# Last layer's probabilities turned by VectorE and SBUF-to-SBUF transfers instead of by TensorE, and new step orders

## The chip, the cores and the metric

The kernel runs on one core of a Trainium2 chip. The metric is the device time of one execution in microseconds; lower is better.

## The reference

64 graphs of 256 nodes with 256 channels go through four layers. All share one 256x256 adjacency matrix. After each layer `x = layernorm(x + layer(x))`. The layers, in short:

```python
# layer 0: scores from two projections
e = leaky_relu((x @ W1) @ (x @ W2).T);  h = relu(softmax(mask(e)) @ (x @ W3))
# layer 1: additive scores
h = x @ W; e = leaky_relu(h @ a1 + (h @ a2).T);  h = elu(softmax(mask(e)) @ h)
# layer 2: MLP, unmasked attention over 512 channels, MLP, masked attention
# layer 3: four heads of 64 channels
q, k, v = x @ wq.T + bq, x @ wk.T + bk, x @ wv.T + bv        # split into 4 heads
scores = where(adj == 0, -inf, q @ k.T / 8)
attn = nan_to_num(softmax(scores));  out = (attn @ v) @ wo.T + bo
```

Layer 3 is the one that changes. Per graph it has four matrices of probabilities of 256x256, one per head. The product `attn @ v` needs each of them with the key index on the partitions, so they have to be transposed.

## The kernel before

Each graph's data lies in tiles of 128 partitions: nodes or channels in two tiles (`NT = CT = 2`). Most products run in three matmuls on a high and a low part (`product3`, lines 192 to 199). Each of the five engines has its own program, and each program is a loop over rounds (`run`, lines 21 to 28). A string per engine in `ORDERS` (lines 8 to 14) lists the steps of a round and for each a stage: in round `k` the step `name:s` works on graph `k - s`. So every step of every layer occurs once per round, for graphs that are at different depths, and some eight graphs are under way at once. Within an engine the steps run strictly in the written order; between engines semaphores hold them back.

The steps of layer 3 for one graph are these.

- TensorE `q4`, `k4`, `v4`: the projections; ScalarE and VectorE make high and low parts in `qT`, `kT`, VectorE adds the bias into `v4`.
- TensorE `s40` and `s42` (lines 403 to 420): scores of heads 0 and 1, then 2 and 3, in PSUM banks 7 and 6.
- VectorE `s40` to `s43` (lines 911 to 917): per head, mask and negated maximum; the result goes to the SBUF tile `p4`, which has room for two heads.
- ScalarE `p40` to `p43` (lines 644 to 651): the exponential with its sum, in place.
- VectorE `p40` to `p43` (lines 919 to 923): reciprocal of the sum. GpSimd `d40` to `d43` and `p40` to `p43` (lines 1029 to 1040): the scaling, in place.
- TensorE `t40` to `t43` (lines 422 to 426): four 128x128 transposes per head into PSUM, through `transposes` (lines 210 to 214).
- ScalarE `t40` to `t43` (lines 653 to 657): copy from PSUM to `p4T`.
- TensorE `a4` (lines 428 to 436): 16 matmuls of `v4` with `p4T` into bank 6, then ScalarE and VectorE `a4`, TensorE `y4` (the output projection), VectorE `y4`, `st4`, `ag4`, GpSimd `v4`, VectorE `n4` (the layer norm) and SyncE `st`, the store.

SyncE issues only three transfers per round: `lt` and `lx` load the input (transposed and plain), `st` stores. All have 128 partitions.

Steps of other layers that are named later: `g0`, `h0`, `s0`, `t0`, `a0`, `x0` (layer 0), `h1`, `f1`, `t1`, `a1`, `x1` (layer 1), `m2`, `n2`, `c2`, `r2`, `f2`, `d2`, `v2`, `b2`, `w2`, `m3`, `n3`, `h3`, `f3`, `t3`, `a3`, `o3`, `x3` (layer 2). The steps `t0`, `t1`, `t3`, `x0`, `x1`, `x3` and `o3` of TensorE are transposes of the same kind as `t40`; `c2` and `r2` (`hidden`, lines 306 to 312) have 24 matmuls each; `f1`, `f3`, `b2` spread two columns, `f2` four.

Of the kernel before, what the change touches and what calls it, by code (L numbers as in the profile page):

```python
# [13 lines left out]
}  # L14
# [16 lines left out]
def graph_stack(nc, x, xT, adj, ident_d, weights, out):  # L31
# [21 lines left out]
    with ExitStack() as ctx:  # L53
# [25 lines left out]
        def small(name, *shape):  # L79
# [42 lines left out]
        nmx4 = sb("nmx4", [P, HEADS, NT])  # L122
        p4 = sb("p4", [P, 2, NT, N])
        p4T = sb("p4T", [P, HEADS, NT, N])
        den4 = sb("den4", [P, HEADS, NT])
# [5 lines left out]
        STAGED = ("W1T", "W2T", "W_T", "hand_T")  # L131
        W.update({n: p4T[:, i, :, :] for i, n in enumerate(STAGED)})
        W.update({"mlp2": p4[:, :, :, :].rearrange("p a b n -> p (a b) n"), "mlp1": o1T[0][:, :, :].rearrange("p (a b) n -> p a (b n)", a=2),
                  "wqT": sco[0][:, :, :], "wkT": sco[1][:, :, :], "wvT": sco[2][:, :, :], "W3": act[0][:, :, :],
# [13 lines left out]
 o3_mm o3T o3Th o3Tl h3_mm h3h h3 f3_mm raw2 nmax2 pro2 rden2 proT2_mm proT2h proT2 av3_mm act2 cut3 ex3 cl3 q3 on3_mm r3 y2 mv2 rstd2 xn2 xnT2_mm xnT2h xnT2  # L148
 q4_mm qTh qT k4_mm kTh kT v4_mm v4 sc4_mm nmx4 p4 rd4a rd4 p4n p4T_mm p4T av4_mm o4Th o4T xb4 y4_mm y3 mv3 rstd3 xn3 stored0 stored1""".split()
        S = {n: ctx.enter_context(nc.semaphore("s_" + n)) for n in names}  # L150
        stored = [S["stored0"], S["stored1"]]
        block = ctx.enter_context(nc.Block())

        def wait(eng, sem, n):
# [5 lines left out]
        @block.sync  # L160
        def _(sp):
            for n, w in weights.items():
                if n not in ("fc", "fc_T"):
                    sp.dma_start(W[n][:, :, :], w).then_inc(S["loaded"], 16)
            for i in range(2):
                sp.dma_start(fc_halves[i], weights["fc"][:, 2 * i:2 * i + 2, :]).then_inc(S["loaded"], 16)
            for k in range(HT):
                sp.dma_start(fcT_tiles[k], weights["fc_T"][:, k, :]).then_inc(S["loaded"], 16)
            sp.dma_start(adj_sb, adj).then_inc(S["loaded"], 16)
            sp.dma_start(ident[:, :], ident_d).then_inc(S["loaded"], 16)  # L170

# [12 lines left out]
            run("sp", {"lt": load_x0T, "lx": load_x0, "st": store}, B)
            sp.wait_ge(stored[0], 16 * ((B + 1) // 2))
            sp.wait_ge(stored[1], 16 * (B // 2))

        @block.tensor
        def _(pe):
# [228 lines left out]
            def s42(t):  # L418
                pe.wait_ge(S["p4T"], HEADS * t + 2)
                scores(2)  # L420

            def t4(h):
                def step(t):
                    pe.wait_ge(S["p4n"], HEADS * t + h + 1)
                    transposes(bank[7 - h % 2], p4[:, h % 2, :, :]).then_inc(S["p4T_mm"], 1)
                return step

            def a4(t):
                pe.wait_ge(S["p4T"], HEADS * t + HEADS)
                for c in range(CT):  # L430
                    for k in range(NT):
                        for g in range(2):
                            h = 2 * c + g
                            ins = nc.tensor.matmul(bank[6][g * HD:(g + 1) * HD, c, :], v4[:, k, h * HD:(h + 1) * HD], p4T[:, h, k, :],  # L434
                                                   start=(k == 0), stop=(k == NT - 1))
                ins.then_inc(S["av4_mm"], 1)

            def y4(t):
# [5 lines left out]
                       "m3": m3, "n3": n3, "h3": h3_, "f3": f3, "t3": t3, "a3": a3, "o3": o3, "x3": x3_, "q4": q4, "k4": k4, "v4": v4_, "s40": s40, "s42": s42,  # L444
                       "t40": t4(0), "t41": t4(1), "t42": t4(2), "t43": t4(3), "a4": a4, "y4": y4}, B)

        @block.scalar
        def _(ac):
# [195 lines left out]
            def p4_(h):  # L644
                def step(t):
                    ac.wait_ge(S["nmx4"], HEADS * t + h + 1)
                    for m in range(NT):
                        ins = nc.scalar.activation(p4[:, h % 2, m, :], p4[:, h % 2, m, :], ACT.Exp, scale=-1.0,  # L648
                                                   bias=nmx4[:, h, m:m + 1], accum_out=den4[:, h, m:m + 1])
                    ins.then_inc(S["p4"], 1)  # L650
                return step

            def t4(h):
                def step(t):
                    ac.wait_ge(S["p4T_mm"], HEADS * t + h + 1)
                    copy(p4T[:, h, :, :], bank[7 - h % 2]).then_inc(S["p4T"], 1)
                return step

            def a4(t):
# [7 lines left out]
                       "q4": q4, "k4": k4, "p40": p4_(0), "p41": p4_(1), "p42": p4_(2), "p43": p4_(3),  # L667
                       "t40": t4(0), "t41": t4(1), "t42": t4(2), "t43": t4(3), "a4": a4}, B)

        @block.vector  # L670
        def _(dv):
# [239 lines left out]
            def s4(h):  # L911
                def step(t):
                    dv.wait_ge(S["sc4_mm"], HEADS // 2 * t + h // 2 + 1)
                    for m in range(NT):
                        ins = V.tensor_tensor_reduce(p4[:, h % 2, m, :], bank[7 - h % 2][:, m, :], mask3[:, m, :], -1.0, BIG, ALU.add, ALU.min, nmx4[:, h, m:m + 1])  # L915
                    ins.then_inc(S["nmx4"], 1)
                return step

            def p4_(h):
                def step(t):  # L920
                    dv.wait_ge(S["p4"], HEADS * t + h + 1)
                    V.reciprocal(den4[:, h, :], den4[:, h, :]).then_inc(S["rd4a"], 1)  # L922
                return step

# [16 lines left out]
            def n4(t):  # L941
                dv.wait_ge(S["rstd3"], 3 * t + 3)
                for m in range(NT):
# [142 lines left out]
```

## Time and profile before

| | us |
|---|---|
| median of 3 runs (lowest, highest) | 3012.59 (3006.74, 3022.74) |
| profiled execution | 3014.59 |
| its span, first to last instruction | 3012.8 |
| TensorE busy | 2812.3 |
| VectorE busy | 2116.2 |
| ScalarE busy | 2101.1 |
| GpSimd busy | 1501.1 |

The mean granted clock of TensorE is 0.98 of full speed. In the lists of groups a row names the line, the engine, the operation, the output and inputs, the shape and the count, then the busy time, the mean duration of one in ns, and the idle time before it with what ended it. The time inside a program that runs for thousands of microseconds is best read in one round of the steady part.

### The profile page before, as it was taken

The page shows a single profiled execution, that of the slowest core. Times are in us where ns is not written, and L with a number is a line of the kernel's source. Part 1 is how long each engine was busy: PE and PEld are TensorE (multiplying, and loading weights), DVE is VectorE, ACT ScalarE, POOL GpSimd, SP SyncE. Part 2 cuts the span into 40 slices and gives each one's busy share as a digit, 9 for nine tenths or more (in the row PEclk, how much of TensorE's full clock was granted, in tenths as well). Part 3 has the DMA queues.
Part 4 walks back from the last instruction along what each step waited for, and adds up shares of the span by engine and source line. Part 5 has one row for each costly group of instructions (what it writes and reads, how often), then busy time and mean ns, then how long its engine had stood idle before and what let it go on. Part 6 is the DMA issues. An engine that isn't in the chain of part 4 may idle for free.

```text
span 3012.8 us, 62503 instructions
## 1 busy us (share of the span) xinstructions
PE 2812.3 (93%) x23496; PEld 2665.5 (88%) x23496; DVE 2116.2 (70%) x5995; ACT 2101.1 (70%) x5057; POOL 1501.1 (50%) x2119
## 2 busy tenths in 40 slices
PE   4689999999999999999999999999999999999886
PEld 3689999999999999999999999999999999998874
DVE  3357777777777777777777777777777777777664
ACT  1367777777777777777777777777777777776663
POOL 0245555555555554555555555555555545554442
PEclk8899999999999999999999999999999999999997
DMA  3000000000000000000000000000000000000000
GB/s 106 22 15 19 15 19 22 22 15 19 22 15 19 22 15 22 19 22 15 19 22 15 19 22 21 16 19 22 16 18 22 15 22 19 22 15 8 8 8 11
DMA packets 40606, 60.98 MB, mean 20 GB/s; under 512 B 4592, under 2 KB 21360, under 8 KB 40304
## 3 DMA queue, kind: packets, MB, share of 16 engines
q1 hardware_dynamic: 40304, 56.98, 5.7%
q8 instruction: 186, 3.05, 0.4%
q14 instruction: 116, 0.95, 0.1%
HBM read 40.19 MB, written 16.78 MB: 19 GB/s over the span
## 4 chain that ended last, share of the span: by engine, by line
PE 84%; DVE 11%; ACT 2%; issue 1%; POOL 1%; SPq 0%; DMA 0%; POOLq 0%; DVEq 0%; ACTq 0%
PE ps L197 41%; PE ps L213 8%; PE ps L206 6%; PE ps L351 6%; PE ps L310 6%; PE ps L311 6%; PE ps L434 4%; DVE xn L944 3%; PE ps L219 2%; PE ps L333 2%; PE ps L409 2%; DVE act L782 2%; DVE o3Tp_lo L675 1%; DVE pfc L817 1%; DVE act L787 1%
## 5 line engine op out<-in xcount | busy, mean ns | idle before, releaser
L963 POOL TENSOR_TENSOR o1Tp_lo<-o1T,o1Tp_hi 128x1024 fp32r<-128x1024 f32 x64 | 162.0, 2531 | 441.1 <-ACT o1Tp_hi L450 441.1
L915 DVE CUSTOM_DVE_ANT_0 p<-ps,mask 128x256 f32<-128x256 f32 x512 | 194.4, 418 | 143.2 <-PE ps L409 143.2
L1032 POOL TENSOR_TENSOR rd<-some,den 128x2 f32<-128x2 f32 x256 | 87.2, 340 | 395.9 <-DVE den L922 395.7
L1038 POOL TENSOR_TENSOR p<-p,rd 128x512 f32<-128x512 f32 x256 | 267.1, 1043 | 15.6
L648 ACT ACTIVATE p<-p,nmx 128x256 f32<-128x256 f32 x512 | 255.0, 505 | 10.2 <-DVE nmx L915 10.2
L717 DVE CUSTOM_DVE_ANT_0 sco<-ps,mask 128x256 f32<-128x256 f32 x384 | 145.8, 417 | 134.8 <-ACT ps L453 134.8
L450 ACT ACTIVATE xnT_hi<-ps 128x512 fp32r<-128x512 f32 x192 | 115.7, 603 | 178.4 <-PE ps L213 178.4
L975 POOL TENSOR_SCALAR xn<-act,nmean,rstd 128x256 f32<-128x256 f32 x384 | 210.7, 558 | 29.6 <-POOL rstd L970 22.4
L213 PE MATMUL ps<-ident,sco 128*128 128x128 f32 x768 | 123.4, 284 | 75.9 <-ACT sco L458 75.6
L458 ACT ACTIVATE sco<-sco,nmax 128x256 f32<-128x256 f32 x384 | 191.3, 517 | 3.6 <-DVE nmax L717 3.6
L675 DVE TENSOR_TENSOR xnT_lo<-ps,xnT_hi 128x512 fp32r<-128x512 f32 x192 | 130.6, 680 | 81.7 <-ACT xnT_hi L450 81.5
L970 POOL TENSOR_TENSOR rstd<-vare,mhalf 128x2 f32<-128x2 f32 x256 | 181.8, 710 | 0.0
L996 POOL TENSOR_TENSOR act<-act,xn 128x512 f32<-128x512 f32 x64 | 88.8, 1387 | 174.7 <-DVE act L782 174.7
L213 PEld LDWEIGHTS ps<-ident,sco 128*128 128x128 f32 x768 | 83.7, 141 | 100.6 <-ACT sco L458 92.5
L450 ACT ACTIVATE h_hi<-ps 128x512 fp32r<-128x512 f32 x192 | 113.8, 593 | 83.9 <-PE ps L206 49.4
L213 PE MATMUL ps<-ident,p 128*128 128x128 f32 x1024 | 156.8, 276 | 15.7 <-POOL p L1038 15.7
L450 ACT ACTIVATE p4T<-ps 128x512 f32<-128x512 f32 x256 | 153.9, 603 | 12.3 <-PE ps L213 12.3
L197 PE MATMUL ps<-xnT_lo,w_mlp_hi 128*128 128x256 f32 x512 | 155.3, 303 | 6.3 <-ACT o1T L539 3.4
L453 ACT ACTIVATE ps<-ps,cols 128x256 f32<-128x256 f32 x384 | 155.4, 450 | 3.0 <-PE ps L219 3.0
L450 ACT ACTIVATE hfc_hi<-ps 128x512 fp32r<-128x512 f32 x128 | 76.5, 598 | 113.0 <-PE ps L311 113.0
L967 POOL TENSOR_TENSOR vare<-mv,eps 128x2 f32<-128x2 f32 x256 | 49.9, 195 | 205.9 <-DVE mv L729 205.9
L197 PE MATMUL ps<-pfcp_lo,hfc_hi 128*128 128x256 f32 x512 | 150.9, 295 | 0.0
(250 smaller groups left out, 12968.1 us busy)
## 6 DMA issues: line engine op xcount, KB each, us to landing
x0T<-in_xT SPq DMA_DIRECT2D x64, 256.0 KB, 3.0
x<-in_x SPq DMA_DIRECT2D x64, 256.0 KB, 2.7
out<-xn SPq DMA_DIRECT2D x64, 256.0 KB, 2.2
o1T<-in_mlp SPq DMA_DIRECT2D x1, 512.0 KB, 4.7
p<-in_mlp SPq DMA_DIRECT2D x1, 512.0 KB, 4.6
att<-in_fc SPq DMA_DIRECT2D x1, 512.0 KB, 5.3
ex<-in_fc SPq DMA_DIRECT2D x1, 512.0 KB, 6.3
xn<-in_fc_T SPq DMA_DIRECT2D x2, 256.0 KB, 6.5
```

What stands on the lines that cost most here:

```text
L197: ins = nc.tensor.matmul(dst[:, m, :], lhs[a][:, k, (off + m) * P:(off + m + 1) * P], rhs[b][:, k, :], start=(k == 0 and i == 0), stop=(k ...
L206: ins = nc.tensor.matmul(dst[m][:, 0:C2], lhs[a][:, k, m * P:(m + 1) * P], rhs[b][:, k, :], start=(k == 0 and i == 0), stop=(k == CT - 1 a ...
L213: ins = nc.tensor.transpose(dst[:, b, a * P:(a + 1) * P], src[:, a, b * P:(b + 1) * P], ident[:, :])
L310: nc.tensor.matmul(ps[:, 4, 0:C2], lhs, WP["fc"][b][:, k, 0:C2], start=(k == 0 and i == 0), stop=(k == HT - 1 and i == 2))
L311: ins = nc.tensor.matmul(ps[:, 5, 0:C], lhs, WP["fc"][b][:, k, C2:], start=(k == 0 and i == 0), stop=(k == HT - 1 and i == 2))
L450: return nc.scalar.activation(dst, src, ACT.Copy)
L458: ins = nc.scalar.activation(sco[i][:, m, :], sco[i][:, m, :], ACT.Exp, scale=-1.0, bias=nmax[i][:, m:m + 1], accum_out=den[i][:, m:m + 1])
L648: ins = nc.scalar.activation(p4[:, h % 2, m, :], p4[:, h % 2, m, :], ACT.Exp, scale=-1.0, bias=nmx4[:, h, m:m + 1], accum_out=den4[:, h, m ...
L915: ins = V.tensor_tensor_reduce(p4[:, h % 2, m, :], bank[7 - h % 2][:, m, :], mask3[:, m, :], -1.0, BIG, ALU.add, ALU.min, nmx4[:, h, m:m + 1])
L970: G.tensor_tensor(rstd[i][:, :], vare[i][:, :], mhalf[:, :], ALU.pow).then_inc(s_rs, 1)
L975: ins = G.tensor_scalar(xn[:, m, :], y[:, m, :], nmean[i][:, m:m + 1], rstd[i][:, m:m + 1], ALU.add, ALU.mult)
L1038: G.tensor_tensor(p4[:, h % 2, :, :], p4[:, h % 2, :, :], rd4[:, h, :].unsqueeze(2).broadcast_to([P, NT, N]), ALU.mult).then_inc(S["p4n"], 1)
```

## The change

Heads are handled in pairs, with one `p4` tile per pair. Within a tile the data is laid out in four blocks of 256 columns, one per quarter of the key index. VectorE transposes all 32x32 blocks of such a tile in place with one instruction (steps `x40` and `x42`, 128x1024 values each). Sixteen transfers issued by SyncE (`i40` and `i42`) then move the 32 partitions of quarter `q`, column block `w`, to the partitions of quarter `w`, column block `q`, of `p4T`. Each moves 32 rows of 1 KB. TensorE's `t40` to `t43` and ScalarE's `t40` to `t43` are gone. TensorE's `s42` waits for the maxima of heads 0 and 1, `a4` for the transfers of each pair. Matmuls and elementwise steps read and write through rearranged views. The orders of all five engines are new.

```diff
 ORDERS = {
-    "sp": "st:9 lx:1 lt:0",
-    "pe": "t3:6 a0:1 s42:7 a3:6 o3:6 d2:5 g0:0 b2:5 v2:5 w2:5 t42:7 x1:4 h0:0 t43:7 m2:4 a4:7 s0:0 x3:6 n2:4 y4:7 q4:6 h1:3 k4:6 m3:5 n3:5 f1:3 x0:2 v4:6 c2:4 s40:6 t1:3 h3:5 t0:0 r2:4 f3:5 t40:6 a1:3 f2:4 t41:6",
+    "sp": "lt:0 i40:7 st:9 lx:1 i42:7",
+    "pe": "h3:8 a0:3 v4:9 f3:8 x0:5 g0:2 s40:9 d2:7 x1:6 t3:8 s42:9 v2:7 a3:8 m2:6 h0:2 b2:7 n2:6 o3:8 w2:7 s0:2 h1:5 c2:6 f1:5 t0:2 a4:9 r2:6 t1:5 x3:8 y4:9 m3:7 n3:7 a1:5 f2:6 q4:8 k4:8",
+    "ac": "t0:3 r2:7 x3:9 m3:8 o3:8 a1:6 f2:7 q4:9 k4:9 h3:8 w2:7 x2:7 a0:3 u3:8 x0:5 p3:8 g0:2 p40:9 t3:8 x1:6 p41:9 p42:9 a3:8 p43:9 m2:6 b3:8 b2:7 h0:2 n2:6 o2:6 s0:2 h1:5 y2:7 p0:2 c2:6 k2:7 u1:5 a4:9 p1:5 z2:7 l0:1 t1:5",
+    "dv": "e0:1 st3:7 h1:4 st0:2 n2:6 ag3:7 ag0:2 c2:5 i2:6 e1:4 j2:6 a4:8 z2:6 x3:7 i1:4 t1:4 i0:1 ag4:9 y4:8 r2:5 t0:1 f2:5 st4:8 b1:4 a1:4 b2:5 q4:7 st1:4 ag1:4 h3:6 k4:7 v4:7 e3:6 x0:3 s40:7 s41:7 g0:0 p40:7 t3:6 s42:7 x1:4 p41:7 i3:6 s43:7 p42:7 d2:5 n4:9 c3:6 p43:7 x40:7 b3:6 h0:0 x42:7 a3:6 r3:6 v2:5 z3:6",
+    "po": "n1:5 d40:8 p40:8 d41:8 p41:8 d42:8 p42:8 d43:8 p43:8 m2:5 a0:2 v3:7 n3:7 v0:2 l0:0 k4:8 v4:9 m3:6 y1:4 n0:2 v1:4 w2:5",
...
-        p4 = sb("p4", [P, 2, NT, N])
-        p4T = sb("p4T", [P, HEADS, NT, N])
+        p4 = [sb(f"p4_{i}", [P, QUADS, 2 * NT * CT * P // QUADS]) for i in range(2)]
+        p4T = sb("p4T", [P, 2, QUADS, 2 * NT * CT * P // QUADS])
+        p4v = [p4[i][:, :, :].rearrange("p w (g a b j) -> p g a w b j", g=2, a=NT, b=CT) for i in range(2)]
+        p4Tv = p4T[:, :, :, :].rearrange("p c q (g a b i) -> p c g b a q i", g=2, a=NT, b=NT)
...
+            def turn_in(c):
+                def step(t):
+                    sp.wait_ge(S["p4x"], 2 * t + c + 1)
+                    wait(sp, S["av4_mm"], t)
+                    for w in range(QUADS):
+                        for q in range(QUADS):
+                            sp.dma_start(p4T[w * QP:(w + 1) * QP, c, q, :], p4[c][q * QP:(q + 1) * QP, w, :]).then_inc(p4Tin[c], 16)
+                return step
...
             def s42(t):
-                pe.wait_ge(S["p4T"], HEADS * t + 2)
+                pe.wait_ge(S["nmx4"], HEADS * t + 2)
                 scores(2)
 
-            def t4(h):
-                def step(t):
-                    pe.wait_ge(S["p4n"], HEADS * t + h + 1)
-                    transposes(bank[7 - h % 2], p4[:, h % 2, :, :]).then_inc(S["p4T_mm"], 1)
-                return step
-
             def a4(t):
-                pe.wait_ge(S["p4T"], HEADS * t + HEADS)
+                pe.wait_ge(S["nmx4"], HEADS * t + HEADS)
                 for c in range(CT):
+                    pe.wait_ge(p4Tin[c], 16 * QUADS * QUADS * (t + 1))
                     for k in range(NT):
                         for g in range(2):
                             h = 2 * c + g
-                            ins = nc.tensor.matmul(bank[6][g * HD:(g + 1) * HD, c, :], v4[:, k, h * HD:(h + 1) * HD], p4T[:, h, k, :],
+                            ins = nc.tensor.matmul(bank[6][g * HD:(g + 1) * HD, c, :], v4[:, k, h * HD:(h + 1) * HD], p4Tv[:, c, g, k, :, :, :],
...
             def s4(h):
                 def step(t):
                     dv.wait_ge(S["sc4_mm"], HEADS // 2 * t + h // 2 + 1)
+                    wait(dv, p4Tin[h // 2], 16 * QUADS * QUADS * t)
...
+            def turn4(c):
+                def step(t):
+                    dv.wait_ge(S["p4n"], HEADS * t + 2 * c + 2)
+                    V.transpose(p4[c][:, :, :], p4[c][:, :, :]).then_inc(S["p4x"], 1)
+                return step
```

## Rows read from the trace of the kernel before

**Rows 1.** The page: busy time by engine, and the chain that ended last.
```profile
PE 2812.3 (93%) x23496; PEld 2665.5 (88%) x23496; DVE 2116.2 (70%) x5995; ACT 2101.1 (70%) x5057; POOL 1501.1 (50%) x2119
...
PE 84%; DVE 11%; ACT 2%; issue 1%; POOL 1%; SPq 0%; DMA 0%; POOLq 0%; DVEq 0%; ACTq 0%
```

**Rows 2.** Busy time in a stretch: PE, PEld, DVE, ACT, POOL, clock, DMA share, GB/s.
```profile
400.00:2400.00 2000.00, 1942.03 (x16562) 1851.88 (x16562) 1480.69 (x4214) 1482.54 (x3581) 1065.39 (x1496) 1.00 0.06 19
```

**Rows 3.** The chain in order of time, one round: start us, us, what.
```profile
1499.39 0.91 PE ps L409 x12
...
1506.30 1.42 PE ps L197 x12
...
1509.97 1.63 DVE xn L944 x2
...
1514.98 1.02 PE ps L333 x8
...
1522.84 0.44 PE ps L213 x4
...
1524.71 1.88 PE ps L434 x16
1526.59 1.61 PE ps L197 x12
...
1535.80 2.82 PE ps L351 x24
1538.62 0.22 PE ps L219 x2
...
1543.57 0.91 PE ps L409 x12
```

**Rows 4.** TensorE's instructions in order of time: start, us, then the idle time before.
```profile
1509.63 0.66 PE L213 MATMUL ps<-ident,sco 128*128 128x128 f32 x4 [1.03 <-ACT sco L458]
```

**Rows 5.** The page's costliest groups, those of layer 3's probabilities.
```profile
L915 DVE CUSTOM_DVE_ANT_0 p<-ps,mask 128x256 f32<-128x256 f32 x512 | 194.4, 418 | 143.2 <-PE ps L409 143.2
...
L1038 POOL TENSOR_TENSOR p<-p,rd 128x512 f32<-128x512 f32 x256 | 267.1, 1043 | 15.6
L648 ACT ACTIVATE p<-p,nmx 128x256 f32<-128x256 f32 x512 | 255.0, 505 | 10.2 <-DVE nmx L915 10.2
...
L213 PE MATMUL ps<-ident,p 128*128 128x128 f32 x1024 | 156.8, 276 | 15.7 <-POOL p L1038 15.7
L450 ACT ACTIVATE p4T<-ps 128x512 f32<-128x512 f32 x256 | 153.9, 603 | 12.3 <-PE ps L213 12.3
```

**Rows 6.** VectorE's groups by shape, 1500 to 2100 us: those of 128x1024.
```profile
L836 DVE SCALAR_TENSOR_TENSOR att<-att,o1T 128x1024 f32<-128x1024 f32 x13 | 15.8, 1215 | 0.0
...
L832 DVE TENSOR_SCALAR ex<-ex 128x1024 f32<-128x1024 f32 x14 | 10.0, 712 | 7.4 <-ACT ex L575 7.4
```

**Rows 7.** SyncE's queue: duration of issues (min/median/max), their starts, landing.
```profile
L178 SPq DMA_DIRECT2D x<-in_x x64: 327/328/609, 17.8 to 2719.9; - x64
L182 SPq DMA_DIRECT2D out<-xn x64: 372/395/403, 274.6 to 3010.2; - x64
...
11.41 0.43 SPq L164 DMA_DIRECT2D w_m<-in_m  x1
11.88 0.43 SPq L166 DMA_DIRECT2D att<-in_fc  x1
12.36 0.43 SPq L166 DMA_DIRECT2D ex<-in_fc  x1
...
1527.29 0.33 SPq L178 DMA_DIRECT2D x<-in_x  x1
1527.66 0.43 SPq L174 DMA_DIRECT2D x0T<-in_xT  x1
...
out<-xn SPq DMA_DIRECT2D x64, 256.0 KB, 2.2
...
w_m<-in_m SPq DMA_DIRECT2D x1, 0.5 KB, 4.3
```

More of the change, by code:

```diff
@@ L46, in graph_stack @@
     HD = C // HEADS
+    QUADS = 4
+    QP = P // QUADS
     MASK = -(2.0 ** 100)
@@ L131, in graph_stack @@
         STAGED = ("W1T", "W2T", "W_T", "hand_T")
-        W.update({n: p4T[:, i, :, :] for i, n in enumerate(STAGED)})
-        W.update({"mlp2": p4[:, :, :, :].rearrange("p a b n -> p (a b) n"), "mlp1": o1T[0][:, :, :].rearrange("p (a b) n -> p a (b n)", a=2),
+        p4T_flat = p4T[:, :, :, :].rearrange("p c q n -> p (c q n)").rearrange("p (h t n) -> p h t n", h=HEADS, t=CT)
+        W.update({n: p4T_flat[:, i, :, :] for i, n in enumerate(STAGED)})
+        W.update({"mlp2": p4[0][:, :, :], "mlp1": o1T[0][:, :, :].rearrange("p (a b) n -> p a (b n)", a=2),
                   "wqT": sco[0][:, :, :], "wkT": sco[1][:, :, :], "wvT": sco[2][:, :, :], "W3": act[0][:, :, :],
@@ L148, in graph_stack, with by_quads @@
  o3_mm o3T o3Th o3Tl h3_mm h3h h3 f3_mm raw2 nmax2 pro2 rden2 proT2_mm proT2h proT2 av3_mm act2 cut3 ex3 cl3 q3 on3_mm r3 y2 mv2 rstd2 xn2 xnT2_mm xnT2h xnT2
- q4_mm qTh qT k4_mm kTh kT v4_mm v4 sc4_mm nmx4 p4 rd4a rd4 p4n p4T_mm p4T av4_mm o4Th o4T xb4 y4_mm y3 mv3 rstd3 xn3 stored0 stored1""".split()
+ q4_mm qTh qT k4_mm kTh kT v4_mm v4 sc4_mm nmx4 p4 rd4a rd4 p4n p4x p4T0 p4T1 av4_mm o4Th o4T xb4 y4_mm y3 mv3 rstd3 xn3 stored0 stored1""".split()
         S = {n: ctx.enter_context(nc.semaphore("s_" + n)) for n in names}
         stored = [S["stored0"], S["stored1"]]
+        p4Tin = [S["p4T0"], S["p4T1"]]
         block = ctx.enter_context(nc.Block())
+        def by_quads(row):
+            return row.rearrange("p (b w j) -> p w b j", b=CT, w=QUADS)
         def wait(eng, sem, n):
@@ L182, in store @@
                 sp.dma_start(out[t].rearrange("(t p) c -> p t c", p=P), xn3[t % 2][:, :, :]).then_inc(stored[t % 2], 16)
-            run("sp", {"lt": load_x0T, "lx": load_x0, "st": store}, B)
+            def turn_in(c):
[6 more added lines that the diff above has]
+                return step
+            run("sp", {"lt": load_x0T, "lx": load_x0, "st": store, "i40": turn_in(0), "i42": turn_in(1)}, B)
             sp.wait_ge(stored[0], 16 * ((B + 1) // 2))
@@ L408, in scores @@
                             rows_ = slice((g % 2) * HD, (g % 2) * HD + HD)
-                            ins = nc.tensor.matmul(bank[7 - g % 2][:, m, :], qT[a][rows_, g // 2, m * P:(m + 1) * P], kT[b][rows_, g // 2, :],
+                            ins = nc.tensor.matmul(bank[7 - g % 2][:, m, :], qT[a][rows_, g // 2, m * P:(m + 1) * P], by_quads(kT[b][rows_, g // 2, :]),
                                                    start=(i == 0), stop=(i == 2))
@@ L444, in _ @@
                        "m3": m3, "n3": n3, "h3": h3_, "f3": f3, "t3": t3, "a3": a3, "o3": o3, "x3": x3_, "q4": q4, "k4": k4, "v4": v4_, "s40": s40, "s42": s42,
-                       "t40": t4(0), "t41": t4(1), "t42": t4(2), "t43": t4(3), "a4": a4, "y4": y4}, B)
+                       "a4": a4, "y4": y4}, B)
         @block.scalar
@@ L647, in step @@
                     for m in range(NT):
-                        ins = nc.scalar.activation(p4[:, h % 2, m, :], p4[:, h % 2, m, :], ACT.Exp, scale=-1.0,
+                        rows_ = p4v[h // 2][:, h % 2, m, :, :, :].rearrange("p w b j -> p w (b j)")
+                        ins = nc.scalar.activation(rows_, rows_, ACT.Exp, scale=-1.0,
                                                    bias=nmx4[:, h, m:m + 1], accum_out=den4[:, h, m:m + 1])
                     ins.then_inc(S["p4"], 1)
[L651 to L656, printed above, removed]
                 return step
@@ L667, in _ @@
                        "q4": q4, "k4": k4, "p40": p4_(0), "p41": p4_(1), "p42": p4_(2), "p43": p4_(3),
-                       "t40": t4(0), "t41": t4(1), "t42": t4(2), "t43": t4(3), "a4": a4}, B)
+                       "a4": a4}, B)
         @block.vector
@@ L678, in _ @@
             V.tensor_scalar(mask16[:, :, :], adj_sb, 0.0, MASK, ALU.is_le, ALU.mult)
-            V.tensor_scalar(mask3[:, :, :], adj_sb, 0.0, MASK, ALU.is_equal, ALU.mult).then_inc(S["setup_dve"], 1)
+            for m in range(NT):
+                ins = V.tensor_scalar(mask3[:, m, :].rearrange("p (w b j) -> p w b j", w=QUADS, b=CT), by_quads(adj_sb[:, m, :]), 0.0, MASK, ALU.is_equal, ALU.mult)
+            ins.then_inc(S["setup_dve"], 1)
             dv.wait_ge(S["setup_dve"], 1)
@@ L913, in step @@
                     dv.wait_ge(S["sc4_mm"], HEADS // 2 * t + h // 2 + 1)
+                    wait(dv, p4Tin[h // 2], 16 * QUADS * QUADS * t)
                     for m in range(NT):
-                        ins = V.tensor_tensor_reduce(p4[:, h % 2, m, :], bank[7 - h % 2][:, m, :], mask3[:, m, :], -1.0, BIG, ALU.add, ALU.min, nmx4[:, h, m:m + 1])
+                        ins = V.tensor_tensor_reduce(p4v[h // 2][:, h % 2, m, :, :, :].rearrange("p w b j -> p w (b j)"), bank[7 - h % 2][:, m, :].rearrange("p (w n) -> p w n", w=QUADS),
+                                                     mask3[:, m, :].rearrange("p (w n) -> p w n", w=QUADS),
+                                                     -1.0, BIG, ALU.add, ALU.min, nmx4[:, h, m:m + 1])
                     ins.then_inc(S["nmx4"], 1)
@@ L950, in _ @@
                        "q4": q4, "k4": k4, "v4": v4_, "s40": s4(0), "s41": s4(1), "s42": s4(2), "s43": s4(3),
-                       "p40": p4_(0), "p41": p4_(1), "p42": p4_(2), "p43": p4_(3), "a4": a4, "y4": y4, "st4": st4, "ag4": ag4, "n4": n4}, B)
+                       "p40": p4_(0), "p41": p4_(1), "p42": p4_(2), "p43": p4_(3), "x40": turn4(0), "x42": turn4(1), "a4": a4, "y4": y4, "st4": st4, "ag4": ag4, "n4": n4}, B)
         @block.gpsimd
@@ L1037, in step @@
                     po.wait_ge(S["rd4"], HEADS * t + h + 1)
-                    G.tensor_tensor(p4[:, h % 2, :, :], p4[:, h % 2, :, :], rd4[:, h, :].unsqueeze(2).broadcast_to([P, NT, N]),
-                                    ALU.mult).then_inc(S["p4n"], 1)
+                    rows_ = p4v[h // 2][:, h % 2, :, :, :, :].rearrange("p a w b j -> p a w (b j)")
+                    G.tensor_tensor(rows_, rows_, rd4[:, h, :].unsqueeze(2).unsqueeze(3).broadcast_to([P, NT, QUADS, CT * QP]), ALU.mult).then_inc(S["p4n"], 1)
                 return step
```

3 rows, old and new, of the table ORDERS are left out of this document.

## The prediction

> **What bounds the kernel now.** I read four views. First the page: TensorE is busy for 93% of the span and carries 84% of the chain that ended last, VectorE 11% of it [rows 1]. Then a long stretch from the middle: in 2000 us TensorE is busy for 1942 us and VectorE for 1481, ScalarE for 1483, GpSimd for 1065, at a granted clock of 1.00, the 2.4 GHz level [rows 2]. So this is TensorE's queue with three engines at some three quarters, and what counts is one round: the time from one graph's `s40` to the next one's, 1499.39 to 1543.57, is 44.2 us [rows 3]. 64 rounds are 2828 us; the other 185 us of the 3012.8 us span are the setup and the rounds at both ends.
>
> The same rows give the price of each TensorE step: a product of 12 matmuls 1.43 us (1.42 to 1.61 with what precedes it), a step of four transposes 0.44, a pair of columns spread 0.22, `d2` 1.02, the scores of a pair of heads 0.91, `a4` 1.88, `m3` with `n3` 2.82. A `hidden` step is 24 matmuls of 0.12 us, 2.9 us. One round without a wait is then 14 products 20.0, `h1` and `h3` 2.9, `m3`/`n3` 2.8, `c2` and `r2` 5.8, scores 1.8, `a4` 1.9, eleven transposing steps 4.8, spreads 1.1, `d2` 1.0: 42.1 us. The remaining 2.1 us are waits, such as 1.03 us of `t1` for the exponentials [rows 4], and a stretch of the chain that runs over VectorE's `n4` at 1509.97 [rows 3].
>
> **What the change removes.** `t40` to `t43` on TensorE: four steps of 0.44 us, 1.8 us per round (all 1024 transposes together are 156.8 us busy, with overlaps [rows 5]). That work is on the path. The four copies of 0.60 us on ScalarE [rows 5] go too; ScalarE is at 74%, so by themselves they bring nothing. The round's TensorE work is then 40.3 us. If nothing waited, 3.9 us per round would be gone, 8%.
>
> **What it adds on VectorE.** Two transposes over 128x1024 float32. No row shows one. The nearest rows of the same size are 0.71 us (one tensor and a scalar) and 1.22 us (two tensors) [rows 6]. I take 1.2, as each element is moved at least once; the ends are 0.7 and 2.4 (two passes). VectorE goes from 33 to 35.4 us busy per round, still under 40.3. The Trainium skill, Vector Engine (DVE) Microarchitecture Reference, section 3.8, says that the array sustains one element per cycle per lane; by that the estimate stays at the row of one element per cycle. No run here shows it yet.
>
> **What it adds on the queue of SyncE.** 32 transfers per round of 32 rows by 1 KB, 1 MB in all; the 16 DMA engines are 6% busy [rows 2], so bytes are no matter. What matters is that one queue issues them one after another. The trace has three prices for an issue: a load alone 0.328 us (64 times), a store alone 0.395 (64 times), and `x0T` right behind `x` 0.37 from start to start; in the setup, with a queue of some twenty, 0.475 from start to start, whether 0.5 KB or 512 KB are moved [rows 7]. So size is not what costs. Fewer rows might: the store has twice the rows of the load (1 KB pieces against 2 KB) and costs 0.07 more, by which a quarter of the rows would take 0.05 off, 0.32 with the gap of 0.045. I take 0.40 us per transfer, between 0.37 and 0.475 and nearer the lower end; bounds 0.32 and 0.475. Sixteen take 6.4 us. Landing: the store of 256 KB takes 2.2 us from issue [rows 7]; 32 KB should be a little quicker, 2.0 (1.8 to 2.2).
>
> **The step that decides: from `s42` to `a4`.** `a4` waits for `i40`'s transfers before its first half and for `i42`'s before its second. Both halves hang on `s42` of the same graph in the same round of TensorE's order, so no earlier start of the round absorbs a delay. Time 0 is the end of `s42`.
> VectorE: it is by then through `s40`, `s41`, `g0` and `t3`; masked maximum of head 2 (0.42 us each half [rows 5], 0.7 us per head with overlap) done at 1.0.
> ScalarE: finishes `p41` at 1.15, `p42` (two exponentials of 0.505 [rows 5] and the sums, 0.98) at 2.1. Then `a3` stands in its queue, which needs TensorE's `v2` and `a3`, 2.9; it is done at 3.7. `p43` at 4.7.
> VectorE: `n4` (1.63 [rows 3]), `c3`, reciprocal of head 3 at 4.9; only then `x40`, although its input (GpSimd's 1.04 us products [rows 5]) is ready at about 3.1. `x40` ends at 6.1. `x42`, behind `b3` and `h0`, ends at 8.6.
> SyncE: `i40` issues from 6.1 to 12.5; `st` and `lx`, 0.8 with their gaps, to 13.3; `i42` starts its last transfer at 13.3 + 15 x 0.40 = 19.3, landed at 21.3. `x42` isn't the limit; the queue is.
> TensorE reaches `a4` after `v2 a3 m2 h0 b2 n2 o3 w2 s0 h1 c2 f1 t0`: eight steps of 12 matmuls 11.4, `c2` 2.9, two spreads 0.4, two transposing steps 0.9, 15.6; the second half starts 0.9 later, at 16.5. The first half's transfers land at 6.1 + 6.0 + 2.0 = 14.1 and are in time. The second half waits 21.3 - 16.5 = 4.8 us.
> The other new waits cost nothing by this: `s42` waits for the maxima of heads 0 and 1 instead of two copies; VectorE's `s40` to `s43` wait for the transfers of the graph before to have read `p4`, done some 20 us earlier; SyncE's wait in `i40` holds `st`, `lx` and `i42` behind it, all of which have slack except `i42`. The setup's mask in two instructions is below 1 us, once.
> Behind the wait of `a4` stand, on TensorE, `r2`, `t1`, `x3`, `y4`; on ScalarE `a4`, and behind it `p1`, `z2`, `l0`; on VectorE `a4`, `z2`, `x3`. I followed them round with the same prices: `p1` is done 1.7 us after `a4`, hidden by `r2` (2.9); `t1` on VectorE is done before `a1`; `z2` just before `m3`. No second wait of more than some tenths comes out; the closest are `s42` behind the maxima of heads 0 and 1 and `c2` behind GpSimd's `m2`. `lt` of the next graph goes out right after `i42`, at about 20.3, lands at 23.3, and `l0` comes on ScalarE at about 25: hidden by 2 us; without that cover it would hold `t1`.
>
> **The sum.** Round: 40.3 + 4.8 = 45.1 us against 44.2, +0.9 us; 64 rounds, +58. In the last two rounds TensorE has few other steps and the new path, some 8 us longer than copies behind transposes, lies open: +15. The profiled execution took 3014.6 us (span 3012.8; the median of three is 3012.6): 3014.6 + 73 = about 3090 us.
> With an issue at 0.37 the wait is 3.9 and the round 44.2: 3030. At 0.475 and a landing of 2.2: `i42` starts at 14.5, lands at 23.8, wait 7.3, round 47.6: 3245. At 0.32 and 1.8: 18.6, wait 2.1, round 42.4: 2914. The break-even of a round is 0.37 us per transfer.
>
> **Rivals.**
> A. *Issues are cheap for small transfers.* If cost followed the rows moved, 32 of 128 rows would cost 0.43 / 4 = 0.11 us, `i42` would start with `x42`'s end at 8.7 and land at 12.4, before 16.5. The round is 40.3 plus half of today's waits, 41.4: -2.8 x 64 + 15, 2850 us. Against it: 0.5 KB costs as much as 512 KB, and 256 pieces little more than 128 [rows 7]. For it: no row has 32 partitions. The Trainium skill, DMA: Bandwidth & Descriptors, section Issuing engines are not separate DMA queues, calls the sequencer's time to initiate a DMA "usually small relative to the DMA itself"; by that this rival is right, while the 0.4 us beside 2.2 here, sixteen times, speaks against it. The same page's Rules for kernel authors say that transfers under 64 KB pay mostly overhead and should be joined; by that my forecast is right. Chance 0.15; a middle case, 0.2 to 0.35 us per issue, 2860 to 2990 us, 0.10.
> B. *VectorE becomes the bound.* At 2.4 us per transpose `x40` ends 1.2 later and the issues with it: round 46.3, 3165 us. It decides from the point where `x42` and the steps behind it (`a3 r3 v2 z3 e0`) reach ScalarE's `p0` later than `t0`, which has some 0.5 us to spare, so also by contention of GpSimd with transposes. Chance 0.08, slower.
> C. *The matmuls pay for the new layout.* `s40`, `s42` and `a4` now read their moving side in runs of 32 floats. At half as much again, 0.9 + 0.9 us: 1.8 per round on TensorE, 0.9 of it hidden in the wait; about 3150. Nothing in the trace speaks for it. Chance 0.03. That the change doesn't take the transposes off TensorE can't be: the steps are gone.
> D. The forecast, 0.64: 0.37 to 0.475 us per issue, 3030 to 3245, and a small part below.
>
> **Chances and range.** Measurable is about 0.5%, 15 us. Faster: A 0.15, the middle case 0.09, a part of D 0.02, 0.26. Within 0.5%: 0.08, the lower end of D and 0.01 of the middle. Slower: the rest of D 0.55, B and C 0.11, 0.66. The range leaves out the cheapest issues below (A) and 0.475 with more waits above: 2890 to 3250. Likeliest, by D alone, 3030 to 3245.
>
> **What would show it.** In the profile after: the distance between two issues of `i40` (0.40 us) and from the last issue to its landing (2.0); the wait of the matmul with `v` and `p4T` for a transfer, about 4.8 us in each round, and a share of it in the chain with DMA and SyncE's queue; VectorE's transpose 1.2 us; rounds of 45.1 us; granted clock 1.00 as before. The prediction is wrong if `a4` doesn't wait (issues under 0.3 us), if `x40` ends much later than 6 us after `s42`, or if another step waits longer than `a4`.

## The result, and the profile after

The kernel after takes 3749.84 us (median of 4 runs, 3745.8 to 3753.1) against 3015.49 us. The ratio is 1.244, 95% interval 1.240 to 1.247: 24% slower, far outside 2890 to 3250. The direction was forecast; the size was not.

The page of the kernel after: busy time, granted clock, and the chain that ended last by engine and by line.

```profile
span 3746.8 us, 62818 instructions
PE 2823.9 (75%) x22472; PEld 2641.0 (70%) x22472; DVE 2282.2 (61%) x6124; ACT 1998.7 (53%) x4801; POOL 1552.0 (41%) x2119
...
PE 50%; SPq 34%; issue 5%; DVE 4%; ACT 3%; DMA 3%; POOL 1%; POOLq 0%; DVEq 0%
SPq L201 32%; PE ps L217 23%; PE ps L371 5%; PE ps L330 4%; PE ps L233 4%; PE ps L449 3%; PE ps L331 3%; DMA p4T<-p 3%; PE ps L429 3%; PE ps L226 2%; DVE p L943 2%; ACT p L664 2%; PE ps L353 2%; PE ps L239 1%; SPq L193 1%
...
L449 PE MATMUL ps<-p4T,v 128*64 128x256 f32 x1024 | 210.8, 551 | 814.8 <-DMA p4T<-p 814.8
```

TensorE had 84% of the chain in [rows 1]; now the queue of SyncE has 34%, nearly all of it in one line, the issue of the small transfers (L201). The last line says what TensorE pays: before `a4` it waits 814.8 us for these transfers, 12.7 us per round. TensorE's own instructions in the round shown next split this wait over the two halves of `a4`; the first half waits too:

```profile
1642.69 1.48 PE L449 MATMUL ps<-p4T,v 128*64 128x256 f32 x8 [2.79 <-DMA p4T<-p]
1653.84 1.98 PE L449 MATMUL ps<-p4T,v 128*64 128x256 f32 x8 [9.68 <-DMA p4T<-p]
```

The chain in order of time, one round, answers to [rows 3] (columns: start, us, what):

```profile
1623.13 0.91 PE ps L429 x12
1624.03 3.06 PE ps L217 x24
...
1627.49 0.47 ACT act L633
1627.96 0.98 ACT p L664 x4
1628.97 0.17 DVE den L937
1629.13 1.15 DVE p L943
1630.30 0.51 SPq L201
1630.86 0.59 SPq L201
1631.49 0.59 SPq L201
...
1636.85 1.29 SPq L201
...
1641.34 0.58 SPq L193
1641.97 0.47 SPq L189
...
1651.33 0.59 SPq L201
1651.97 1.83 DMA p4T<-p
1653.84 1.98 PE ps L449 x8
...
1659.39 0.87 PE ps L233 x8
```

This is the path of the prediction, step by step: scores of `s42` to 1624.03, then `v2` and `a3`, ScalarE's `a3` and `p43`, the reciprocal, `x40`, sixteen issues, store and load, sixteen issues, one landing, `a4`. `x40` ends 6.3 us after `s42`; 6.1 was forecast. But an issue lasts 0.59 us, 0.635 from start to start, not 0.40; 37 of the 2048 last over 1 us. The second half of `a4` starts 29.8 us after `s42`, not at 21.3.

The same stretch by windows (busy PE, PEld, DVE, ACT, POOL; granted clock; DMA share; GB/s):

```profile
1624.00:1641.00 17.00, 15.90 (x134) 15.66 (x132) 13.83 (x35) 11.86 (x31) 6.95 (x8) 1.00 0.11 29
1641.00:1654.00 13.00, 1.63 (x10) 0.76 (x12) 5.45 (x15) 1.85 (x3) 5.81 (x9) 0.59 0.33 89
1654.00:1658.00 4.00, 4.00 (x22) 2.86 (x23) 0.69 (x1) 2.13 (x6) 0.00 (x0) 0.64 0.19 54
1658.00:1679.00 21.00, 21.00 (x188) 20.57 (x188) 15.06 (x44) 15.02 (x37) 11.33 (x16) 1.00 0.01 2
```

While TensorE waits, its granted clock falls from 2.4 to 1.2 GHz, and it still runs at the lower level for the first steps after the wait (0.64 in the third window). The eight matmuls of `a4` take 1.98 us there, and 16 took 1.88 in [rows 3]. [Rows 2] had 1.00.

A mean round is used below. It is the mean of 50 rounds from the middle: the start of `a4`'s second half of the 56th graph less that of the 6th, over 50. In the kernel after these are 3322.28 and 542.38, so 55.6 us; in the kernel before 2674.30 and 465.26, so 44.2. (The last rounds, in which the first layers have nothing left to do, are shorter and are left out.) Over the same 50 rounds the second half of `a4` starts 29.5 us after `s42` in the kernel after, 28.9 to 30.3.

### The profile page after: what moved, and what is told of

It is laid out like the page before. It is cut to its first block, busy times and chain, and to the rows that moved or that the text cites. A ratio compares the mean times of both kernels' runs of the same rounds, so it can differ in the third digit from the quotient of the medians.

```text
span 3746.8 us, 62818 instructions
## 1 busy us (share of the span) xinstructions
PE 2823.9 (75%) x22472; PEld 2641.0 (70%) x22472; DVE 2282.2 (61%) x6124; ACT 1998.7 (53%) x4801; POOL 1552.0 (41%) x2119
## 4 chain that ended last, share of the span: by engine, by line
PE 50%; SPq 34%; issue 5%; DVE 4%; ACT 3%; DMA 3%; POOL 1%; POOLq 0%; DVEq 0%
SPq L201 32%; PE ps L217 23%; PE ps L371 5%; PE ps L330 4%; PE ps L233 4%; PE ps L449 3%; PE ps L331 3%; DMA p4T<-p 3%; PE ps L429 3%; PE ps L226 2%; DVE p L943 2%; ACT p L664 2%; PE ps L353 2%; PE ps L239 1%; SPq L193 1%
## 5 line engine op out<-in xcount | busy, mean ns | idle before, releaser
L449 PE MATMUL ps<-p4T,v 128*64 128x256 f32 x1024 | 210.8, 551 | 814.8 <-DMA p4T<-p 814.8
L449 PEld LDWEIGHTS ps<-p4T,v 128*64 128x64 f32 x1024 | 90.0, 184 | 898.0 <-DMA p4T<-p 671.4
L735 DVE BATCH_NORM_STATS2 stat<-act 128x6 f32<-128x256 f32 x384 | 143.9, 416 | 419.8 <-POOL act L1006 414.8
L465 ACT ACTIVATE qT_hi<-ps 128x512 fp32r<-128x512 f32 x64 | 38.3, 598 | 486.8 <-PE ps L449 486.8
L594 ACT ACTIVATE ex<-ex,w_m 128x1024 f32<-128x1024 f32 x64 | 73.5, 1148 | 419.9 <-DVE ex L844 419.9
L984 POOL TENSOR_TENSOR x0Tp_lo<-x0T,x0Tp_hi 128x512 fp32r<-128x512 f32 x64 | 111.9, 1749 | 434.8 <-ACT x0Tp_hi L465 434.8
L1006 POOL TENSOR_TENSOR act<-act,x 128x512 f32<-128x512 f32 x64 | 81.4, 1271 | 496.6 <-DMA x<-in_x 486.3
L988 POOL TENSOR_TENSOR vare<-mv,eps 128x2 f32<-128x2 f32 x256 | 107.9, 422 | 412.7 <-DVE mv L741 412.7
L685 DVE TENSOR_TENSOR qT_lo<-ps,qT_hi 128x512 fp32r<-128x512 f32 x64 | 44.3, 692 | 379.1 <-ACT qT_hi L465 379.1
L330 PE MATMUL ps<-w_fc_lo,o1Tp_hi 128*128 128x258 f32 x512 | 177.6, 347 | 8.5 <-POOL o1Tp_lo L984 5.9
```

The costliest lines, as they stand in the source:

```text
L330: nc.tensor.matmul(ps[:, 4, 0:C2], lhs, WP["fc"][b][:, k, 0:C2], start=(k == 0 and i == 0), stop=(k == HT - 1 and i == 2))
L984: return G.tensor_tensor(lo, whole, hi.bitcast(fp32), ALU.subtract)
```

## The experiments

A run that is given without a ratio was executed once.

**One transfer of sixteen.** The wait at `a4` is the suspect; this takes away what it waits for.

```diff
-for w in range(QUADS):
-    for q in range(QUADS):
-        sp.dma_start(...)
+for i in range(1):          # eight in the second run; waits count accordingly
+    w, q = i // QUADS, i % QUADS
+    sp.dma_start(...)
```

> Kernel after with one of the sixteen transfers of each pair of heads (30 of the 32 per round left out, so most of p4T keeps old values); transposes, new orders and new views stay. Theory Q (the wait of a4 for SyncE's 16 + 16 issues at 0.635 us from start to start makes the slowdown): the second pair is landed at about 9 + 0.6 + 1.8 = 11.4 us after s42, before a4 needs it at 16.5; rounds of 40.3 to 41.5 us, granted clock 1.00, about 2840 to 2910 us. Rival V (VectorE's transposes, the new order or matmuls that read in runs of 32 are slow by themselves): it stays above 3015 us, with another wait or longer matmuls.

Measured: 2800.28 us, ratio to before 0.928 (0.923 to 0.934). In the steady part TensorE has no idle time left (the columns are those of [rows 2]):

```profile
800.00:2400.00 1600.00, 1600.00 (x13745) 1539.26 (x13745) 1375.47 (x3739) 1226.66 (x2954) 971.01 (x1295) 1.00 0.08 22
```

The mean round is 40.8 us, 0.5 more than the prediction's sum of TensorE's steps and with no wait in it; a matmul of `a4` takes 0.379 us as in the kernel before. Transposes on VectorE, new orders, and matmuls that read in runs of 32 cost nothing on the path; rival V falls. The whole loss comes with the other 30 transfers.

**Eight of sixteen.**

> Kernel after with eight of the sixteen transfers per pair (half of p4T keeps old values). Theory Q: i40 issues from 6.25 to 11.3, st and lx to 12.5, the last of i42 starts at 16.9 and lands at 18.7, a wait of 2.2 us at a4: rounds of 42.5 to 43.5 us, 2980 to 3040 us. Rival V: hardly different from the run with one transfer.

3047.06 us, just above the range named; mean round 44.7 us. The wait at `a4` is 2.4 us per round in the middle, against 2.2 expected. The clock makes most of the rest: it is 0.96 in the steady part, and the expectation had left it out. From the start of `a4`'s second half to the steps of L233 it is 5.2 us in the mean, against 3.9 in the run with one transfer. In 36 of the 50 rounds this stretch is over 5 us, behind waits of only 1.8 to 3.1 us; in the other 14 it is 4.0.

**What sets the price of an issue: fewer bytes, more partitions.** Two runs change the shape alone.

```diff
-p4T[w*QP:(w+1)*QP, c, q, :],      p4[c][q*QP:(q+1)*QP, w, :]
+p4T[w*QP:(w+1)*QP, c, q, 0:64],   p4[c][q*QP:(q+1)*QP, w, 0:64]      # 32 rows of 256 B
+p4T[:, c, q, w*64:(w+1)*64],      p4[c][:, w, q*64:(q+1)*64]         # 128 rows of 256 B
```

> Kernel after, all 32 transfers per round, but each of its 32 rows is 256 bytes instead of 1 KB (three quarters of p4T keep old values). If an issue has a price per instruction: still 0.59 us each, about 3750 us. If the price follows the bytes: under 0.3 us each, landing under 1.8, rounds near 41 us, about 2870 us. If only the landing shrinks: some 20 us less.

> Kernel after, all 32 transfers per round with the same 32 KB each, but as 128 rows of 256 bytes over all partitions (the blocks don't go to their places, so the output is of wrong probabilities). If the 32-partition shape is what makes an issue 0.59 us instead of the 0.43 us of the loads in the setup: 0.43 us each, 0.475 from start to start, a wait of about 7 us, 3250 us. If it is that both ends lie in SBUF, or that many follow one another: 0.59 us, about 3750 us. If more rows cost more: above 3750 us.

3746.96 and 3758.67 us. The issues in the first, the second, and for comparison the run with one transfer (durations in ns, min/median/max):

```profile
L201 SPq DMA_DIRECT2D p4T<-p x2048: 507/591/1935, 243.2 to 3730.2; - x187
```
```profile
L201 SPq DMA_DIRECT2D p4T<-p x2048: 464/601/1748, 243.9 to 3741.8; - x187
```
```profile
L193 SPq DMA_DIRECT2D out<-xn x64: 378/584/1440, 322.2 to 2793.4; - x64
L201 SPq DMA_DIRECT2D p4T<-p x128: 507/513/1301, 240.1 to 2781.1; - x128
```

A quarter of the bytes, 0.591 us as in the kernel after; four times the rows and partitions, 0.601. So it is a price per instruction. Nor is it the length of the queue: with a single transfer per pair it is 0.51 us, and the store right behind it takes 0.58, against 0.395 in [rows 7].

**The same transfers with one end in device memory.**

```diff
-p4[c][q*QP:(q+1)*QP, w, :]
+xT[t][q*QP:(q+1)*QP, c, :]
```

> Kernel after with the same 32 transfers of 32 rows by 1 KB to the same places in p4T, but read from the input in device memory instead of from p4 (so the probabilities are left out of the product). Theory E (an issue whose both ends lie in SBUF costs 0.59 us, one with an end in device memory 0.43): 0.475 us from start to start; i40 from 6.25 to 13.9, st and lx to 14.9, the last of i42 starts at 22.0 and lands near 24.4, a wait of 7.9 us and the lower clock behind it, rounds of 48.5 to 50 us, 3300 to 3400 us. If it is the number of rows or partitions: 0.59 us and 3750 us as after.

3426.62 us; the issues in the same form, and the first of a round by time:

```profile
L201 SPq DMA_DIRECT2D p4T<-in_xT x2048: 310/421/1952, 242.5 to 3409.9; - x187
```
```profile
1607.06 0.31 SPq L201
1607.41 0.42 SPq L201
1607.88 0.42 SPq L201
...
1623.28 1.70 DMA p4T<-in_xT
1625.02 1.97 PE ps L449 x8
...
1631.81 0.87 PE ps L233 x8
```

0.42 us instead of 0.59, 0.465 from start to start, with the same 32 rows to the same places. What makes an issue dear here is that both its ends lie in SBUF. The time is a little above the range named: mean round 50.4 us. From the start of `a4`'s second half to the steps of L233 it takes 6.8 us in the round shown and 6.1 in the mean of the 50 (5.4 to 6.9), where a full clock needs 3.9 to 4.0 (below). The lower clock costs 2.2 us per round here.

**Keeping the clock up.** 90 matmuls stand ahead of the second wait.

```diff
+if c == 1:
+    for _ in range(90):
+        nc.tensor.matmul(bank[6][:, 1, :], WP["wvT"][0][:, 0, 0:P], WP["wvT"][0][:, 1, :], start=True, stop=True)
 pe.wait_ge(p4Tin[c], 16 * QUADS * QUADS * (t + 1))
```

> Kernel after with 90 matmuls of 256 columns put in front of a4's wait for the second pair (their result is overwritten, so the output is kept). They take 10.6 us in which TensorE otherwise waits. Theory C (besides the wait of 12.7 us per round, TensorE's clock falls behind each wait and costs another 1.8 us: rounds of 55.3 us less 12.7 are 42.6, while the run with one transfer has 40.8): clock 1.00, rounds of about 53.5 to 54 us, 3630 to 3670 us. If the 1.8 us are other waits: 3750 us as after, or more.

3719.34 us, ratio to before 1.234 (1.231 to 1.237), so 31 us below the kernel after, not 80 to 120. The chain:

```profile
1630.51 1.83 DMA p4T<-p
...
1632.48 1.08 PE ps L452 x8
1633.56 10.98 PE ps L447 x90
1644.55 1.01 PE ps L452 x8
...
1648.62 0.87 PE ps L233 x8
```

The eight matmuls behind the fill take 1.01 us instead of 1.98, and 4.1 us pass until the steps of L233 where the round shown of the kernel after needs 5.5. That round is one of the mild ones: from start to start the stretch is 4.0 us in each of the 50 rounds with the fill and 6.0 in the mean of the kernel after (5.4 to 6.9). So the clock costs 2.1 us per round there. But the first half of `a4` itself waited for its transfers until 1632.48, and the fill started late. The matmuls behind it started 0.3 us after the last transfer's landing in this round and 1.0 in the mean (0.04 in the kernel after), and the issues of the second pair took 0.4 us longer than in the kernel after, so that the mean round fell by only 0.7 us, to 54.9. The price of the clock is shown by the rows; its gain in this run is smaller by the overshoot and the issues.

**The two issues between the pairs.**

```diff
-"sp": "lt:0 i40:7 st:9 lx:1 i42:7"
+"sp": "lt:0 lx:1 i40:7 i42:7 st:9"
```

> Computes the full result. Kernel after with SyncE's order changed alone: lx before i40 and st behind i42, so that nothing stands between the 32 issues. Theory Q: every round loses the 1.2 us of these two issues from the chain: 54.1 us, about 3675 us. If the queue is not the chain, no change from 3750. VectorE's long idle stretch behind GpSimd's wait for x (7.8 us per round) should go as well; if that was what cost, more than 1.2 us per round goes.

3695.03 us, 55 below the kernel after, where 75 were expected; the mean round is 54.6, 1.0 less. The second half of `a4` starts 1.1 us earlier, by the length of the two issues, and the stretch at the lower clock behind it is 0.1 longer. Two issues that leave the queue between the pairs give nearly their own length, as a queue on the path must. `stat L735 <- POOL act`, up to 7.8 us per round in the middle and 414.8 us in all, went out of VectorE's waits and gave nothing of its own; VectorE's wait for `qT_hi` grew from 379 to 731 us.

**More cover for the same 32 transfers.**

```diff
 "pe": ... t0:2 r2:6 t1:5 x3:8 m3:7 n3:7 a4:9 a1:5 f2:6 y4:9 q4:8 k4:8    # a4 7 us later
 "ac": t0:3 r2:7 x3:9 m3:8 o3:8 a4:10 a1:6 f2:7 ...                       # a4 moved to the start of the next round
 "dv": ... p42:7 d2:5 x40:7 n4:9 c3:6 p43:7 ...                           # x40 ahead of n4; a4, y4, st4 later
 "sp": lt:0 lx:1 i40:7 i42:7 st:9                                         # first run
 "sp": lt:0 lx:2 i40:8 i42:8 st:10                                        # second: all but lt a stage later, so lt a round earlier than the rest
```

> Computes the full result. All 32 transfers as in after, but more cover: TensorE's a4 moved behind r2, t1, x3, m3, n3 (7 us later in the round), y4 behind f2, VectorE's x40 ahead of n4 (1.8 us earlier), SyncE as in the run with its order changed. Theory Q: i40 issues from 4.4 to 15.2 us after s42, the last of i42 starts at 24.7 and lands at 26.5; a4's second half could start at 23.4: a wait of 3.1 us and the lower clock behind it, rounds of 44 to 46 us, 3000 to 3130 us, no better than before. If it stays above 3500 us, the number of issues isn't what holds it.

3478.5 us, not 3000 to 3130, and just below the 3500 above which the number of issues would not have been what holds it. `a4` hardly waits any more (59.7 us in all), but something else does. Its chain, from the last issues on:

```profile
1660.39 0.59 SPq L201
1660.99 0.04 issue
1661.03 0.58 SPq L193
1661.62 0.04 issue
1661.66 2.67 DMA x0T<-in_xT
...
1664.89 0.58 ACT proT_hi L465
...
1667.73 0.60 DVE proT_lo L685
1668.32 0.04 issue
1668.37 2.93 PE ps L217 x12
```

The load of `x0T` stands behind the 32 issues. ScalarE's `l0` waits for it and holds `t1`, `a1` waits for that. This is the cover of 2 us that the prediction named at `l0`; with `a4` off the path it is used up. The second run puts the load ahead.

> Computes the full result. The kernel with the later a4, and the load of x0T one round earlier in SyncE's order, so that it goes out before i40 and not behind the 32 issues. In the run before, the chain went from the last issue over the landing of x0T (2.7 us), ScalarE's queue and VectorE's proT and xnT back to TensorE, and a4 waited only 60 us in all. If that is the whole reason why later didn't reach 3000 to 3130 us: it does now, with a4's wait of about 3 us per round back. If VectorE or ScalarE is out of order for another reason: it stays above 3300 us.

3097.74 us, inside 3000 to 3130 at the second attempt. The remaining waits are not where they were expected: 60.8 us at `a4`, 96.1 for `o2T` and 61.5 for `hfc`, 3.4 us per round together; the mean round is 45.0. So with the same 32 transfers the kernel is 24% or 3% slower than the kernel before, by where their consumer and the load behind them stand.

**Fewer issues, through device memory.** This computes the whole result.

```diff
+def turn_out(c):            # i40, i42
+    sp.dma_start(scratch[c], p4[c][:, :, :]).then_inc(p4out[c], 16)
 def turn_in(c):             # j40, j42, after p4out[c]
     for w in range(QUADS):
-        for q in range(QUADS):
-            sp.dma_start(p4T[w*QP:(w+1)*QP, c, q, :], p4[c][q*QP:(q+1)*QP, w, :]).then_inc(p4Tin[c], 16)
+        sp.dma_start(p4T[w*QP:(w+1)*QP, c, :, :], scratch[c][:, w, :].rearrange("(q j) n -> j q n", q=QUADS)).then_inc(p4Tin[c], 16)
-"sp": "lt:0 i40:7 st:9 lx:1 i42:7"
+"sp": "lt:0 i40:7 st:9 lx:1 i42:7 j40:7 j42:7"
```

> Computes the full result. Kernel after, but the blocks of a pair change places through device memory: one transfer of 128 partitions writes the turned tile out, four transfers of 32 partitions read it back, 10 issues per round instead of 32, with one landing more in the way (2.5 and 2.9 us). Theory Q (number of issues, not bytes or distance): i42 goes out at 8.9 us after s42, has landed at about 11.5, the last read starts at about 13.5 and lands at 16.4, just when a4 needs it at 16.5. Rounds of 40.8 to 41.5 us, 2800 to 2850 us, against 3015 before. If the round trip through device memory takes over 2 us more than that: a wait and a lower clock again, over 2950 us. It also shows whether an issue between device memory and SBUF with 32 partitions costs 0.43 or 0.59 us.

2873.41 us, ratio to before 0.954 (0.951 to 0.956), a little above the 2800 to 2850 named. A read back costs 0.43 us again behind another. What is left of the wait at `a4` is 82.5 us, since the landings are longer than assumed (us from issue to landing, last column):

```profile
scratch<-p SPq DMA_DIRECT2D x128, 512.0 KB, 3.4
p4T<-scratch SPq DMA_DIRECT2D x512, 128.0 KB, 3.5
```

**The same with two changes of order.**

```diff
-"sp": "lt:0 i40:7 st:9 lx:1 i42:7 j40:7 j42:7"
+"sp": "lt:0 lx:1 i40:7 i42:7 j40:7 j42:7 st:9"
-"dv": "... x40:7 b3:6 h0:0 x42:7 a3:6 ..."
+"dv": "... x40:7 b3:6 x42:7 h0:0 a3:6 ..."
```

> Computes the full result. The kernel through device memory with two changes of order: VectorE turns the second pair ahead of h0 (x42 some 1.2 us earlier after s42), and SyncE issues lx ahead of i40 and st last, so that the load of x doesn't stand between the two writes. Theory Q: the 1.2 us that a4 still waited per round go: rounds near 40.5 us, 2800 to 2830 us. If s0 now waits for the late h0, or the landings stay at 3.4 and 4.2 us because the bytes of both pairs meet on the DMA engines: 2840 to 2880 us, hardly better than 2873.

2823.45 us, ratio to before 0.936 (0.934 to 0.938), mean round 41.0. It is the fastest kernel of this study that computes the whole result, and 23 us above the run with one transfer, the bound for this path. TensorE is busy all but 6 of 1600 us:

```profile
800.00:2400.00 1600.00, 1593.71 (x13659) 1530.08 (x13658) 1378.62 (x3708) 1217.51 (x2926) 967.11 (x1290) 1.00 0.23 72
```

## Why the prediction was right and wrong

**Right: what is removed, and nearly what the round is without waits.** 40.3 us per round was the sum of TensorE's steps; the run with one transfer has 40.8.

**Right: the place and the path.** The wait that sets the round is at `a4`'s second half, the limit is SyncE's queue and not `x42`, `x40` ends at 6.3 us (6.1), the landing is 1.8 us (2.0), VectorE's transpose 1.23 us (1.2). Rivals B and C are excluded by the run with one transfer, rival A by every trace here. That the first half would be in time was wrong: it waits 2.3 us per round. This costs nothing by itself, as the second half's transfers land some 11 us later still.

**Wrong: the price of an issue.** This is the step that failed. 0.40 us, with bounds 0.32 and 0.475, was taken from transfers of [rows 7] that all have one end in device memory. The rows fit those, as the run from memory shows: 0.465. With both ends in SBUF it is 0.635. The argument that a quarter of the rows would take 0.05 us off gave nothing: a quarter of the bytes left the price where it was, and four times the rows and partitions added 0.01. None of the prediction's three signs of being wrong came true either; they looked at a cheaper issue, a late `x40` and another step, and not at a dearer issue. A term that enters the path 31 times should have had a bound from outside the kinds of transfer that the trace happened to show, and break-even lay at 0.37.

**Wrong: the clock was left out.** A wait of this length lets the granted clock fall to 1.2 GHz, and the work behind it pays: 2.1 us per round here, 2.2 in the run from memory, 1.3 in the one with eight transfers. The prediction said that the clock would stay at 1.00.

**The sum made again.** The run with one transfer needs 24.0 us from the start of `a4`'s second half to the next `s42`'s end. The time lost to the clock is what the stretch from the start of that half to the steps of L233 takes beyond the 3.9 us of that run. In the mean of the 50 rounds the parts add up so (us):

| | second half starts | rest at full clock | clock | sum | measured |
|---|---|---|---|---|---|
| forecast | 21.3 | 23.8 | 0 | 45.1 | |
| after | 29.5 | 24.0 | 2.1 | 55.6 | 55.6 |
| order of the queue | 28.4 | 24.0 | 2.2 | 54.6 | 54.6 |
| from memory | 24.2 | 24.0 | 2.2 | 50.4 | 50.4 |
| eight of sixteen | 19.3 | 24.0 | 1.3 | 44.6 | 44.7 |

The 8.2 us by which the half starts later are 31 issues 0.235 dearer, 7.3; store and load between the pairs 1.2 instead of 0.8, 0.4; the issues of over 1 us, 0.4; `x40` and landing together 0.1. With 2.1 for the clock and 0.2 for the rest the round is 10.5 longer than forecast. Times 64 this is 670 us, where 660 lie between 3090 and 3750; the last rounds are shorter.

So the price of the issues carries most of it. At the forecast price of 0.40 the clock alone would have left the time inside the range: by the 1.3 to 2.2 us of these runs, 3170 to 3230 us, an estimate. Had the issues cost 0.475, the upper bound of the prediction, it would have given 3245. The run from memory, at 0.465, has 3427, and some 140 of these 182 us are the clock.

The Trainium skill, DMA: Bandwidth & Descriptors, section Issuing engines are not separate DMA queues, calls the time to initiate a DMA usually small relative to the DMA itself. The trace agrees for one transfer (0.5 us beside 1.8) and contradicts it for sixteen in a row, where 10 us of issues stand ahead of one landing. Its rule in Rules for kernel authors to join transfers of under 64 KB is borne out by the version through device memory, which moves twice the bytes in a third of the issues.

**Open.** Why an issue takes longer when both ends lie in SBUF, and why a store or load right behind such a one takes 0.58 us too, isn't known. Nor is what makes an issue last over 1 us now and then. How much of the gain of the last version through device memory is the orders and how much the missing transposes wasn't separated, since no run has the new orders with the old transposes: of 3.2 us per round (44.2 to 41.0), by the prediction's prices 1.8 are the transposes, and about 1.4 would be waits that the old order had. No run issued part of the transfers from a second engine's queue either.

## What to carry to other kernels

Many small transfers on one queue are a serial engine with a price per instruction: multiply it by their number, put it on the path, and compare with the cover between the last producer and the first consumer. Count what stands behind them in that queue too; moving the consumer can turn the next load into the new wait. Once a wait of TensorE comes out at some 2 us or more, as in the run with eight transfers, add the time that the lower clock costs behind it. And where bytes are cheap, a detour through device memory in a few large transfers can beat a direct way in many small ones.

## What the runs showed of the hardware that was not expected

- Issue of a transfer from SyncE with one end in device memory: 0.31 to 0.40 us alone, 0.42 to 0.47 behind another such. With both ends in SBUF: 0.51 alone and 0.59 behind another, the same for 8 and 32 KB; for 128 rows of 256 B 0.46 and 0.60.
- The transfer ahead counts as much as the transfer itself: one with an end in device memory takes 0.58 us right behind one inside SBUF, and one inside SBUF only 0.52 right behind one with an end in device memory.
- The lower clock behind a wait cost 2.1 us (kernel after, 10.0 us of wait before the second half), 2.2 (from memory, 7.1 us) and 1.3 (eight transfers, 2.4 us) in the mean, and 1.4 to 2.9 in single rounds of the kernel after.
- A write of 512 KB to device memory and its read in four parts landed after 3.4 and 3.5 us each, with 82 GB/s in the busiest slices of the steady part. TensorE's busy time was 2678 us there and 2668 in the run with one transfer.
